# Six of 49 destination blocks of a graph convolution summed from rows fetched per edge, among the dense blocks

## The reference, cut to what matters

```python
# 6250 nodes x 256, 206250 edges sorted by dst (one loop per node among them), as data
src = concatenate([edge_index[0], arange(N)]); dst = ...       # one more loop per node
norm = dinv[src] * dinv[dst]                                   # dinv = deg ** -0.5
h = x @ W                                                      # x: layer-normalised
out = segment_sum(h[src] * norm[:, None], dst, N) + b
x = x + where(out > 0, out, prelu_a * out)
# then a mixture of experts, the two best of 8 for the whole graph, and a layer norm
```

## Time and profile before

| | us |
|---|---|
| median of 3 runs | 1186.95 |
| lowest and highest | 1186.08, 1187.92 |
| the profiled execution | 1189.44 |
| its span, first to last instruction | 1187.8 |
| PE busy | 1153.4 (97%) |
| DVE busy | 899.3 (76%) |
| ACT busy | 596.9 (50%) |
| POOL busy | 392.0 (33%) |

### The profile page before, as it was taken

One profiled execution on the slowest core, in us unless ns is written; L12 is line 12 of the kernel. 1 busy time (PEld: TensorE's weight loads), 2 busy tenths in 40 slices (PEclk: granted clock), 3 DMA queues, 4 the chain that ended last, 5 costly groups with the idle time before them and its releaser, 6 DMA issues. The chain is left out here.

```text
span 1187.8 us, 25216 instructions
## 1 busy us (share of the span) xinstructions
PE 1153.4 (97%) x7396; PEld 985.8 (83%) x7397; DVE 899.3 (76%) x2049; ACT 596.9 (50%) x1521; POOL 392.0 (33%) x474
## 2 busy tenths in 40 slices
PE   7999999999999999999999999999989999999996
PEld 5777888888888888888888888888868999999996
DVE  7897777777777777787777777878456778788785
ACT  5874444444444444444444444444276455565551
POOL 3101233333333333333333333333313334244331
PEclk9999999999999999999999999999989999999999
DMA  8000000000000000000000000000031111111101
GB/s 273 15 2 3 22 21 21 21 21 19 21 12 21 21 21 21 19 21 12 21 21 21 21 21 20 20 18 13 25 124 39 39 44 40 46 47 40 44 27 32
DMA packets 24257, 38.95 MB, mean 33 GB/s; under 512 B 4100, under 2 KB 18062, under 8 KB 24222
## 3 DMA queue, kind: packets, MB, share of 16 engines
q0 software_dynamic: 8448, 22.87, 6.5%
q1 hardware_dynamic: 15774, 15.65, 4.1%
HBM read 25.68 MB, written 12.82 MB: 32 GB/s over the span
## 5 line engine op out<-in xcount | busy, mean ns | idle before, releaser
L1627 PE MATMUL bank<-tab,adj 128*128 128x512 f32 x2401 | 600.9, 399 | 2.3 <-POOL adj L606 2.3
L1627 PEld LDWEIGHTS bank<-tab,adj 128*128 128x128 f32 x2401 | 437.5, 189 | 91.2 <-issue 2.5
L1373 ACT CAST adj<-bank 128x392 fp32r<-128x392 f32 x768 | 317.2, 501 | 320.9 <-PE bank L1609 320.9
L1003 DVE TENSOR_TENSOR hot_key<-iota_key,turned 128x588 bf16<-128x588 bf16 (+1 forms) x588 | 260.3, 496 | 0.0
L1609 PEld LDWEIGHTS bank<-hot_key,hot_src 128*128 128x128 bf16 x2304 | 193.1, 146 | 50.4 <-issue 49.7
L1609 PE MATMUL bank<-hot_key,hot_src 128*128 128x147 bf16 (+1 forms) x2304 | 227.6, 248 | 0.0
L995 DVE TENSOR_TENSOR hot_src<-iota_src,turned 128x1536 bf16<-128x1536 bf16 x196 | 187.0, 954 | 22.8 <-issue 12.0
L606 POOL TENSOR_TENSOR adj<-adj,ident 128x128 f32 (+1 forms) x49 | 69.4, 1416 | 384.6 <-ACT adj L1373 383.5
L1212 DVE TENSOR_TENSOR gl<-gf,gh 128x384 fp32r<-128x384 f32 (+1 forms) x136 | 117.1, 888 | 29.7 <-ACT gf L1444 29.3
L1442 ACT ACTIVATE gh<-bank,b1e 128x384 fp32r<-128x384 f32 (+1 forms) x136 | 78.2, 575 | 96.6 <-PE bank L1734 96.5
L946 DVE SCALAR_TENSOR_TENSOR agg<-bank,dinv,low_b 128x256 f32<-128x256 f32 x48 | 23.2, 483 | 118.2 <-POOL low_b L569 118.2
(11 more groups left out here) (219 smaller groups left out, 1258.9 us busy)
## 6 DMA issues: line engine op xcount, KB each, us to landing
xin<-in_x POOLq DMA_DIRECT2D x49, 128.0 KB, 2.3
x_dram<-x POOLq DMA_DIRECT2D x49, 128.0 KB, 2.0
x1f<-x_dram POOLq DMA_DIRECT2D x16, 384.0 KB, 3.7
out<-res SPq DMA_DIRECT2D x48, 128.0 KB
xs<-in_x SPq DMA_DIRECT2D x2, 1536.0 KB, 14.5
xs<-in_x SPq DMA_DIRECT2D x1, 1664.0 KB, 15.4
xs<-in_x SPq DMA_DIRECT2D x1, 1024.0 KB, 9.3
dst_all<-in_dst SPq DMA_DIRECT2D x1, 816.0 KB, 4.0
```

What stands on the lines that cost most here:

```text
L1003: v.tensor_tensor(hot_win[s % 2][j], iota_key[:, lo:hi, :].rearrange("p (o n) c -> p o n c", o=1).to_broadcast(shape), turned[:, k, 1, at: ...
L1373: s.copy(adj[k][:, :].rearrange("p (q n) -> p q n", n=P)[:, :, at:at + GN], adj_ps[j][:, 0:KEYS].rearrange("p (n q) -> p q n", q=T)).then_ ...
L1627: last = mm(acc[k][:, :], adj[k][:, q * P:(q + 1) * P], tab[:, q, :], start=(q == 0), stop=(q == T - 1), skip_group_check=True)
```

## The change

Six blocks (10, 17, 24, 31, 38, 45) are no longer dense. The table is also written to DRAM (`h_table`), by SP, in six parts as they are made. The edges of a gathered block are read as a list of 35 x 128 (`load_list`, by SP). For each of 35 chunks POOL issues one indirect DMA that brings, to 128 partitions, the table row of 128 edges' source nodes, 2 KB each, into a ring of seven buffers (`gather`); DVE makes a one-hot 128x128 of the edges' destinations (`hot_rows`); PE multiplies the two into a third PSUM bank, `acc_row` (`add_gathered`). One more matmul with the identity adds the second loop. These 36 matmuls are spread over the rounds of the five dense windows before the block (for block 10 the windows of 5 to 9); the sixth, between two such groups, has none. The epilogue of the gathered block is done beside that of the dense block after it.

All loops over blocks are written out. From block 8 on SP, not POOL, loads the tile of x and stores x1, and POOL does not wait for the stores. The memory of prologue tensors is shared with the ring; b1, gamma and beta are loaded later by SP, when the ring is no longer used. Two small DVE operations and one small matmul in the prologue send a block with more than 4480 edges to the general path.

Of the functions that are written anew the diff shows the new lines only; what they replace stands in the listing above.

```diff
+GCH = 35
+GFROM, GSTEP = 10, 7
+GWIN = GSTEP - 2
+RING = 7
...
+    GATHERED = list(range(GFROM, T - 3, GSTEP))
+    DENSE = [d for d in range(T) if d not in GATHERED]
+    ND, NGATH, ITEMS = len(DENSE), len(GATHERED), GCH + 1
+    BY_SP = 8
+    TABLE_PARTS = ((0, 8), (HELD, 32), (8, 16), (32, 40), (16, HELD), (40, T))
...
+    def items(i, s):
+        for m, d in enumerate(GATHERED):
+            q = (DENSE[i] - (d - GWIN)) * STEPS + s
+            if 0 <= q < GWIN * STEPS:
+                return m, q * ITEMS // (GWIN * STEPS), (q + 1) * ITEMS // (GWIN * STEPS)
+        return 0, 0, 0
+    def chunks(i, s):
+        m, lo, hi = items(i, s)
+        return [m * GCH + j for j in range(lo, hi) if j < GCH]
+    def followers(i, s):
+        return [n + RING for n in chunks(i, s) if n + RING < NGATH * GCH] if i < ND else []
...
                 return t
             return take
+        room = tenants(RING_AT, TAB_AT)
+        row = room("row", [P, RING, 2 * D], F32R)
+        hot_row = room("hot_row", [P, RING, P], F32R)
...
         first_ps = banks[4:7]
+        acc_row = banks[6]
...
+        def low_free(eng, d):
+            eng.wait_ge(low_kept, d + 3)
+            eng.wait_ge(epi, d * EPI + (2 * EPI + 1))
...
             with sp.If(is_dense(sp)):
-                sp.wait_ge(acc_ready, T)
+                for lo, hi in TABLE_PARTS:
+                    if lo < HELD:
+                        sp.wait_ge(lo_fixed, hi)
+                    else:
+                        sp.wait_ge(lo_made, hi - HELD)
+                    sp.dma_start(h_table[lo * P:hi * P, :].rearrange("(t p) d -> p t d", p=P), tab[:, lo:hi, :].bitcast(F32)).then_inc(h_kept, 16)
+                sp.wait_ge(starts_ready, 1)
+                tab_made(sp)
+                for m in range(2):
+                    load_list(m)
+                for d in range(BY_SP - 2, T):
+                    sp.wait_ge(epi, d * EPI + (2 * EPI + 4))
+                    if d >= BY_SP:
+                        sp.dma_start(x1_dram[d * P:(d + 1) * P, :], x1[:, d % 2, :]).then_inc(x1_by_sp[d % 2], 16)
+                    if d + 2 < T:
+                        sp.dma_start(xin[:, d % 2, :], x[(d + 2) * P:(d + 3) * P, :]).then_inc(tile_by_sp[d % 2], 16)
+                    if d in GATHERED[:NGATH - 2]:
+                        m = GATHERED.index(d)
+                        sp.wait_ge(row_used, (m + 1) * GCH)
+                        load_list(m + 2)
+                    if d == GATHERED[-1]:
+                        sp.wait_ge(row_used, NGATH * GCH)
+                        load_late()
+                for d in (T - 2, T - 1):
+                    landed, value = x1_landed(d)
+                    sp.wait_ge(landed, value)
+                sp.sem_inc(x1_out, T)
...
+                def gather(n):
+                    m, c, u = n // GCH, n % GCH, n % RING
+                    if n == 0:
+                        pool.wait_ge(h_kept, 16 * len(TABLE_PARTS))
+                    if c == 0:
+                        pool.wait_ge(list_in[m % 2], m // 2 * 16 + 16)
+                    if n >= RING:
+                        pool.wait_ge(row_used, n - RING + 1)
+                    g.indirect_dma_start(
+                        out=row[:, u, :].bitcast(F32), out_offset=None, in_=h_table,
+                        in_offset=bass.IndirectOffsetOnAxis(ap=lists[:, m % 2, c, 0:1], axis=0),
+                        bounds_check=T * P - 1).then_inc(row_in[u], 16)
+                def ends(i):
+                    d = DENSE[i]
+                    if i + 4 < ND:
+                        load_edges(i + 4)
+                    for n in followers(i, STEPS - 1):
+                        gather(n)
+                    if d < T - 1:
                         add_bias(d)
+                    if d:
+                        add_z(d - 1, (d - 1) % 2, P)
+                    for s in range(STEPS - 1):
+                        for n in followers(i + 1, s):
+                            gather(n)
+                    if d == GFROM - GWIN - 2:
+                        for n in range(RING):
+                            gather(n)
+                    if d + 1 in GATHERED:
+                        add_bias(d + 1)
+                    if i + 2 < ND:
+                        add_loop(i + 2)
+                    if d + 1 in GATHERED:
+                        add_z(d, d % 2, P)
+                    if d < BY_SP:
+                        store_x1(d, d % 2)
+                        if d + 2 < BY_SP:
+                            load_tile(d + 2, d % 2)
+                        landed, value = x1_landed(d)
+                        pool.wait_ge(landed, value)
                 pool.wait_ge(starts_ready, 1)
+                for i in range(3):
+                    load_edges(i)
                 load_tile(0, 0)
                 load_tile(1, 1)
+                load_edges(3)
+                add_loop(0)
+                add_loop(1)
+                for i in range(ND):
+                    ends(i)
+                pool.wait_ge(acc_ready, T)
+                load_x1()
...
+                def hot_rows(i, s):
+                    for n in chunks(i, s):
+                        m, c, u = n // GCH, n % GCH, n % RING
+                        if c == 0:
+                            dve.wait_ge(list_in[m % 2], m // 2 * 16 + 16)
+                            v.tensor_scalar(own_dst[:, :], lists[:, m % 2, :, 1], float(-P * GATHERED[m]), None, ALU.add).then_inc(own_dst_made, 1)
+                            dve.wait_ge(own_dst_made, m + 1)
+                        if n >= RING:
+                            dve.wait_ge(row_used, n - RING + 1)
+                        v.tensor_scalar(hot_row[:, u, :], iota[:, :], own_dst[:, c:c + 1], None, ALU.is_equal).then_inc(hot_row_made, 1)
+                def rows_of(b):
+                    k = b % 2
+                    d = DENSE[b - 2]
+                    beside = b > 2 and d - 1 in GATHERED
                     hot_step(b, k, 0)
+                    if b + 1 < ND:
+                        decode(b + 1)
+                    hot_rows(b - 1, 0)
                     hot_step(b, k, 1)
+                    if b > 2:
+                        x1_norm(DENSE[b - 3], DENSE[b - 3] % 2, 0)
+                    if beside:
+                        x1_sum(d - 1, acc_row)
+                    hot_rows(b - 1, 1)
+                    hot_rows(b - 1, 2)
                     hot_step(b, k, 2)
+                    if beside:
+                        x1_stats(d - 1, (d - 1) % 2, 0)
+                    elif b > 1:
+                        x1_sum(d, acc[k])
+                    hot_rows(b - 1, 3)
                     hot_step(b, k, 3)
+                    if beside:
+                        x1_norm(d - 1, (d - 1) % 2, 0)
+                        x1_sum(d, acc[k])
+                    if b > 1:
+                        x1_stats(d, d % 2, 0)
...
+                def counts(b):
+                    k = b % 2
+                    d = DENSE[b - 2]
+                    beside = b > 2 and d - 1 in GATHERED
+                    if b > 2:
+                        deviation(DENSE[b - 3])
+                    if beside:
+                        keep_low(d - 1, acc_row)
+                    elif b > 1:
+                        keep_low(d, acc[k])
                     for s_ in range(STEPS):
                         keep_counts(b, k, s_)
-                        if s_ == 1 and following:
+                        if s_ == 0 and beside:
+                            keep_low(d, acc[k])
+                        if s_ == 1 and b + 1 < ND:
                             keep_edges(b + 1, 1 - k)
+                        if s_ == 1 and beside:
+                            deviation(d - 1)
...
+                def add_gathered(i, s):
+                    m, lo, hi = items(i, s)
+                    for j in range(lo, hi):
+                        n = m * GCH + j
+                        if j == 0 and m == 0:
+                            pe.wait_ge(consts, N_CONSTS + 1)
+                        if j == 0 and m:
+                            low_free(pe, GATHERED[m - 1])
+                        if j < GCH:
+                            pe.wait_ge(hot_row_made, n + 1)
+                            pe.wait_ge(row_in[n % RING], n // RING * 16 + 16)
+                            mm(acc_row[:, :], hot_row[:, n % RING, :], row[:, n % RING, :], start=(j == 0), stop=False, skip_group_check=True).then_inc(row_used, 1)
+                        else:
+                            mm(acc_row[:, :], ident_r[:, :], tab[:, GATHERED[m], :], start=False, stop=True, skip_group_check=True).then_inc(acc_ready, 1)
+                def window(i):
+                    k = i % 2
                     for s in range(STEPS):
+                        if i and i + 1 < ND:
+                            count_edges(i + 1, s)
+                        if s == 1 and i and i + 2 < ND:
+                            turn_edges(i + 2)
                         if s == 0:
```

(48 more changed lines are left out.)

191 lines of the change are left out of this document (79 added, 112 removed).

## The result

| | kernel before | changed kernel |
| --- | --- | --- |
| median of 4 runs each, same chip, us | 1187.43 | 1150.43 |
| lowest and highest, us | 1186.08 to 1189.11 | 1147.04 to 1152.39 |
| profiled execution, own time and span, us | 1189.44, 1187.8 | 1147.04, 1145.6 |

The ratio is 0.9685, 95% interval 0.9658 to 0.9711. Forecast: 1151, by a sum of -36.3 us; the medians differ by -37.0.

The account below looks back on a forecast made before the run. PE's instruction stream was taken to bound the block loop. Terms of -94.9 - 3.4 + 54.0 + 6 + 2 = -36.3 us gave 1151 us, own range 1143 to 1170, with rival 2 up to 1225.

Parts of the forecast that it names:

- Removed, -94.9 - 3.4: PE: six blocks lose their 15.81 us window, 94.9 us; 23 loop turns of 0.15 us go, 3.4 us.
- Added to PE, +54.0: PE: 216 matmuls for gathered blocks at 0.25 us each, from a span of 0.237 to 0.337, 54.0 us.
- Loop addition after a gathered block, +6: POOL: loop addition queued behind the bias addition, late by 0.2 to 2.2 us; 1.0 taken, six times.
- Start, +2: Table write, first seven gathers in a row ahead of a loop addition, two small operations ahead of the flag: 2 us.
- POOL near its limit: POOL: gather every 1.75 to 1.9 us or slow loop additions; 1166 to 1186 us; chance 12 in 100.
- My sign of being wrong: PE's timeline: the forecast is wrong if windows with gathers are longer than 18.5 us; 17.5 to 17.7 expected.
- The price of a gather: POOL: one indirect DMA of 128 indices takes 1.2 us, between 1.03 and 3.6; every 1.75 or faster fits.
- Rival 2: POOL becomes the bound: 1.93 us per gather means no change, 2.1 gives 1223, 2.5 gives 1307; chance 24 in 100.
- The sum: Whole kernel: -94.9 - 3.4 + 54.0 + 6 + 2 = -36.3 us, to a median of 1151 us.
- my own range: Whole kernel: 1143 (items at 0.237, half the stalls) to 1170 (items at 0.30, 1 to 2 us late after gathered blocks).
- (1): Rival: POOL late by up to 1 us in each of 30 windows with gathers, 15 to 35 us; chance 12 in 100.
- (3): Rival: DVE holds POOL, each gather waits out a DVE group, 2.1 us more, 1433 us; chance 3 in 100.

Follow-up runs that it names:

- the loop addition first: Against SP from block 4 on: loop addition for two blocks on issued ahead of round 2's two gathers, not behind them; 1142.28 us, ratio 0.9617.
- SP from block 4 on: Against the changed kernel: SP stores x1 and loads the next tile from block 4, not block 8; 1146.45 us, ratio 0.9646.
- both additions first: Against the loop addition first: bias addition also ahead of the gathers left from the round before; 1139.28 us, ratio 0.9595.

## Why the prediction was right, step by step

- **Removed, -94.9 - 3.4.** Windows without gathered rows are 15.77 to 15.83 us as read. A turn of the loop cost 0.12 us, not the 0.15 of the one pair I read, so the second term is 2.7; the other 1.9 us by which the first window is shorter go with the granted clock there, and were not in the sum.
- **Added to PE, +54.0.** Measured 0.234 x 216 = 50.6. I had put a price on two met waits per item; there is none to be seen. Too dear by 3.4 us; it is just below the 51 that I had as the lowest.
- **Loop addition after a gathered block, +6.** It costs nothing: PE does not wait for `adj` in the windows that follow a gathered block. ScalarE and POOL there:

```profile
374.75 1.66 ACT L1523 CAST adj<-bank 128x392 fp32r<-128x392 f32 x4 [2.18 <-PE bank L1763]
376.26 0.23 ACT L1511 COPY mean<-mvb 128x1 f32<-128x1 f32 x1
376.36 0.33 ACT L1512 ACTIVATE sd<-mvb,eps 128x1 f32<-128x1 f32 x1
376.55 0.49 ACT L1507 ACTIVATE low<-bank,dinv 128x256 f32<-128x256 f32 x1
377.12 1.06 POOL L668 TENSOR_TENSOR low_b<-low,bias_bc 128x256 f32<-128x256 f32 x1 [8.81 <-ACT low L1507]
378.14 0.69 POOL L706 TENSOR_TENSOR adj<-adj,ident 128x128 fp32r<-128x128 f32 x1
```

PE wants the block at 379.29 (its next row group) and POOL is done at 378.83. The chain I added up is there, but ScalarE's operations overlap: from 374.75 to the start of the bias addition it is 2.37 us, where I had 1.66 + 0.55 + 0.48 + 2 x 0.27 = 3.2. The whole chain took 4.08 us (374.75 to 378.83) of the 4.54 that PE leaves; I had put 4.7 to 6.8. Here the durations of small operations on one engine, added end to end, overstate the chain. This term of the sum failed.
- **Start, +2; POOL near its limit.** The first seven gathers begin at 154.35 with no wait for the table. But stalls of 10.5 us came in its place: 6.9 in the first group, nearly all in the two windows in which POOL still has its own store, load and their landing, and 0.6 to 1.0 in each later group, mostly in its second and third window. I had the pieces (two gathers ahead of the loop addition, a store landing of 1.4 us a window) and costed only the steady window. So 8 us were forecast at wrong places and 10.5 came. My sign of being wrong, windows with gathers over 18.5 us, was met by two of the 30 (18.89 and 22.88).
- **The price of a gather.** I took 1.2 us between 1.03 and 3.6. Unless it is held it is mostly 1.01 to 1.25 and a gap of 0.30 behind the one before, 1.31 to 1.55 of the 1.75 allowed. 128 indices cost what 48 do (least 1.01 and 0.97 us). Rival 2 turned on just this number.
- **The sum.** -94.9 - 2.7 - 1.9 + 50.6 + 10.5 = -38.4 for the blocks; -38.3 was read. The errors of +3.4 and +8 (terms too high or not there) and of -10.5 cancel within a microsecond: the two large terms were right, but that the total is so close is luck. The ends of my own range come out at 1144 and 1168 by the terms that I named for them, not at 1143 and 1170; the result is far inside either. The rest of the profiled -42.2 us of span is the start (+0.6) and the last part (-4.5).
- **The rivals.** (1) came about in part: POOL was late, but by 10.5 us in all and mostly in two windows, not by 15 to 35. (2) did not, but it is near: with nine gathers in a window, or with stores on POOL, the kernel is slower than before. For (3): DVE does hold gathers, 18 of 250 and not each. Why the kernel before did not show it, its trace tells: of its 46 indirect DMAs from 80 us on, 22 began 2.0 us into a group of one-hots and took 1.16, and only one began in the first microsecond of a group. The Trainium skill, page "SBUF — State Buffer", section "SBUF: two separate sides", calls the port pair shared by VectorE and GpSimd an exclusive lock in which the later one waits out the whole instruction. The trace agrees on both sides in part of the cases, 3.13 us instead of 1.01 for a gather and 0.87 instead of 0.41 us for `zst`; but a held gather waits out a group of four instructions, not one. The same page, section "Who interferes with whom", says that a tensor_tensor with both inputs in SBUF contends only with GpSimd instructions that read SBUF, and that its probe saw no DMA stalled by tensor_tensor. `hot_src` and `hot_key` are such operations, and here gathers beside them were held: the measurement decides. The indirect DMA takes its indices from SBUF; that this reading is what is held was not tested. The prediction used the page's rule for two-port modes; whether DVE ran in one here no run shows.

## What to carry to other kernels

When work is put on an engine that already serves others, list each instruction in its queue that somebody waits for, and the latest time of each, and put the fillers behind these. Free time in total (here 12.3 us a window) says little: at the same seven gathers per window the order alone made between 1139 and 1190 us. List too what each of its instructions waits for, since the fillers behind a late wait are late as well (`add_z` above). Fix all deadlines together: taking fillers from one puts them before the next, and the wait that shows up on PE then has another engine's name (`hot_key` of DVE) though POOL's queue is the cause. Cost the odd windows (first, last, and where an old duty still runs) apart from the steady one.

## What the hardware showed beyond this

- An indirect DMA on POOL took 1.01 us at best for 128 indices of 2 KB each and 0.97 for 48, plus a gap of 0.30 us when one follows another.
- One that began between 0.1 us before `hot_src` and 0.75 us after its start (`hot_src` takes 0.95 us, and with the three `hot_key` behind it 2.2 in all) either took 1.0 to 1.7 us or was held, 17 of 86 in the changed kernel: then it took 2.3 to 3.1 us and ended some 0.9 us after the group. In the kernel with the loop addition first, of 48 that began about 0.6 us into `hot_src`, 35 took about 1.2 and 13 up to 2.5. What decides between the two is open.
- Now and then POOL issued nothing for 2.8 us, and I found no cause in the trace (ahead of the gather at 489.62 in the kernel with SP from block 4, at 489.54 in the one with the loop addition first, at 487.13 with both additions first, at 410.99 in the changed one). In the first two this gap and a held gather behind it (2.81 us) stand in the longest window, 23.54 and 21.89 us; with both additions first the window is 18.26, in the changed kernel 17.78. This is open too.
